# Second attention of a two-layer Perceiver block: where the picks, the first maximum and the last scores of a chunk stand

## The reference, cut to what matters

```python
x = x + _L0_xattn_ref(_layernorm(x), ctx_1024, mask, Wq, Wkv, Wo)
x = x + _L0_attn_ref(_layernorm(x), ...)      # gated delta net
x = x + _L0_ffn_ref(_layernorm(x), ...)       # top-1 of 8 experts
# the second attention, _L1_xattn_ref, H = 16 heads, d = 16:
q = (x_1 @ Wq.T + bq).reshape(1, 128, 16, 16).transpose(0, 2, 1, 3)
k = (x_2 @ Wk.T + bk).reshape(1, 12544, 16, 16).transpose(0, 2, 1, 3)
v = (x_2 @ Wv.T + bv).reshape(1, 12544, 16, 16).transpose(0, 2, 1, 3)
scores = einsum('bhqd,bhkd->bhqk', q, k) * 16 ** (-0.5)
out = einsum('bhqk,bhkd->bhqd', softmax(scores), v)
x = x + out
x = x + _L1_attn_ref(_layernorm(x), ...)      # linear attention with decay
x = x + _L1_ffn_ref(_layernorm(x), ...)       # top-2 of 8 experts
```

## Time and profile before

| what | value |
|---|---|
| three runs | 957.21, 960.98 (median), 963.67 us |
| profiled execution | 962.6 us, its span 960.8 us |
| mean granted TensorE clock | 0.984 of full speed |
| TensorE busy | 914.8 us of the span |
| VectorE, ScalarE, GpSimd busy | 709.1, 487.5, 300.2 us |
| second attention, first pick to last value matmul | 588.3 to 924.2 us |

### The profile page before, as it was taken

How to read it: one execution, slowest core, us unless ns; L and a number is a source line. 1 busy time by engine, 2 the same in 40 slices (tenths; PEclk the granted TensorE clock), 3 DMA queues, 4 the chain that set the end, 5 groups by cost and what they waited for, 6 DMA issues and landing times. The chain is left out here.

```text
span 960.8 us, 21439 instructions
## 1 busy us (share of the span) xinstructions
PE 914.8 (95%) x8224; PEld 575.9 (60%) x8224; DVE 709.1 (74%) x1216; ACT 487.5 (51%) x1156; POOL 300.2 (31%) x435
## 2 busy tenths in 40 slices
PE   7999999999999999888999989899999999999987
PEld 5444554455445445555778966566666666666775
DVE  3389778877887798988476625788787878878426
ACT  1543553355345534444386223266666666666743
POOL 4653355435442544356028114400000110000100
PEclk9999999999999999999999979999999999999999
DMA  8377847573557355632310049587766666666100
GB/s 168 132 201 204 226 187 183 136 202 140 130 135 200 127 140 136 159 115 98 106 45 1 2 124 215 138 243 182 178 172 185 161 161 161 167 170 186 48 3 6
DMA packets 103656, 136.33 MB, mean 142 GB/s; under 512 B 64153, under 2 KB 85425, under 8 KB 100881
## 3 DMA queue, kind: packets, MB, share of 16 engines
q1 hardware_dynamic: 99856, 134.22, 51.3%
q10 hardware_dynamic: 3712, 0.92, 0.6%
HBM read 81.48 MB, written 53.07 MB: 140 GB/s over the span
## 5 line engine op out<-in xcount | busy, mean ns | idle before, releaser
L1957 DVE TENSOR_REDUCE mx<-bank 128x1 f32<-128x896 f32 x224 | 233.8, 1085 | 58.3 <-PE bank L1808 55.4
L2018 ACT ACTIVATE p<-bank 128x512 f32<-128x512 f32 x392 | 204.3, 601 | 98.9 <-PE bank L1851 98.4
L699 DVE STREAM_TRANSPOSE ew<-sc 32x896 f32<-32x896 f32 x208 | 229.4, 1103 | 16.8 <-ACT sc L783 7.6
L561 PE MATMUL bank<-Wv,ctxT 128*128 128x512 f32 (+1 forms) x336 | 152.1, 586 | 0.4 <-ACT v L762 0.4
L1851 PE MATMUL bank<-qrows,krows 99*128 99x128 bf16 x1568 | 124.2, 220 | 5.5 <-ACT p L2018 4.8
L1851 PEld LDWEIGHTS bank<-qrows,krows 99*128 99x128 bf16 x1568 | 99.2, 97 | 42.6 <-ACT p L2018 9.7
L1808 PE MATMUL bank<-krows,qrows 96*128 96x512 bf16 x448 | 123.0, 356 | 1.4 <-issue 0.9
L1864 PE MATMUL bank<-p,v 128*32 128x128 f32 x3136 | 108.1, 276 | 4.4 <-issue 4.4
L561 PEld LDWEIGHTS bank<-Wv,ctxT 128*128 128x128 f32 x336 | 60.8, 190 | 79.0 <-issue 48.1
L1864 PEld LDWEIGHTS bank<-p,v 128*32 128x32 f32 x3136 | 80.3, 109 | 39.3 <-ACT p L2018 29.3
L443 POOL CAST kt<-kf 128x512 bf16<-128x512 f32 (+1 forms) x56 | 31.2, 558 | 218.4 <-ACT kf L755 218.4
(11 more groups left out here) (317 smaller groups left out, 1173.0 us busy)
## 6 DMA issues: line engine op xcount, KB each, us to landing
krows<-kscr SPq DMA_DIRECT2D x14, 1536.0 KB, 9.5
krows<-kscr SPq DMA_DIRECT2D x14, 1152.0 KB, 14.6
v<-vscr SPq DMA_DIRECT2D x14, 1004.5 KB, 12.8
vscr<-vpair SPq DMA_DIRECT2D x12, 1004.5 KB, 4.0
kscr<-kt SPq DMA_DIRECT2D x14, 768.0 KB, 3.6
kscr<-kt SPq DMA_DIRECT2D x14, 576.0 KB, 5.1
kscr<-kt SPq DMA_DIRECT2D x14, 512.0 KB, 4.5
ctxB<-ctx SPq DMA_DIRECT2D x56, 112.0 KB, 3.9
```

The lines of the kernel that those rows point to most:

```text
L561: ins = pe.matmul(bank[kv_bank(op, s)][:, 0:w * D], turned_context(c)[:, i, k * P:(k + 1) * P], Wv01[:, i, 0:w].rearrange("p w o -> p (w o)"),
L699: dve.transpose(pT0[j * SQ:(j + 1) * SQ, :, :, i * SQ:(i + 1) * SQ].rearrange("m t h q -> m h t q"), rows[:, j]).then_inc(S("turn0"), 1)
L1957: dve.tensor_reduce(mx1[:, c % 2, h:h + 1], psum[:, b:b + 2, :].rearrange("p b n -> p (b n)")[:, 0:CH], AX.X, ALU.max).then_inc(S("smread1 ...
L2018: act.activation(p1[:, g % PR, :], bank[ST1[g % 3]][:], ACT.Exp).then_inc(S("exp1"), 1)
```

## The change

SPLIT becomes 6, so that the loop scores ten heads one chunk ahead and six two chunks ahead; PLAN1 is written anew. PRO1 has three scores of chunk 1 ahead of the first M, not one, and three behind it, not seven. The third and fourth pick stand between the first scores; each pair of the first eight scores waits for its own cast. The first two late values stand behind the fourth score, with new banks and waits; the fillers begin later. GpSimd builds the mask behind the first maximum.

```diff
--- before.py
+++ after.py
@@ -1628,10 +1628,10 @@
         LATES = (LATE, NCH - 1)
         LU = 2 * CT
         LBANK = (4, 5, 7)
-        LAFTER = (0, 1, 3, 4, 6, 7, 9, 10, 12, 13, 15, 18, 20)
-        LATE_FIRST = 1 + sum(1 for n in LAFTER if n <= H1 + 1)
+        LAFTER = (4, 5, 7, 8, 10, 11, 13, 14, 16, 17, 18, 20)
+        LATE_FIRST = 2 + sum(1 for n in LAFTER if n <= H1 + 2)
         NPICK = 4
-        PBANK = (3, 6, 7, 0)
+        PBANK = (4, 5, 6, 7)
 
         moe0 = experts("moe0", a["L0_ffn_router_w"], True, a["L0_ffn_router_b"], a["L0_ffn_expert_b"], 1, False,
                 l1_loads, l1_clears,
@@ -1643,18 +1643,18 @@
         LB = (6, 7, 0, 1, 2)
         UNITS = CT * H1 // GH
         SLOTS = 3
-        SPLIT = 8
+        SPLIT = 6
 
 
 
         PLAN1 = (
-            (("S8",), ("S9",), ("R",)),
-            (("S10",), ("S11",), ("S12",)),
-            (("S13",), ("S14",), ("S15",)),
-            (("S0",), ("S1",), ()),
-            (("M",), ("S2",), ("S3",)),
-            (("S4",), ("S5",), ()),
-            (("S6",), ("S7",), ()))
+            (("S6",), ("S7",), ("R",)),
+            (("S8",), ("S9",), ("S10",)),
+            (("S11",), ("S12",), ("S13",)),
+            (("S14",), ("S15",), ("S0",)),
+            (("S1",), ("M",), ("S2",)),
+            (("S3",), ("S4",), ()),
+            (("S5",), (), ()))
 
         def plan1(c, t, k):
 
@@ -1671,7 +1671,7 @@
                     if d < NCH:
                         yield "S", d, h
 
-        PRO1 = tuple(("S", 0, h) for h in range(H1)) + (("S", 1, 0), ("M", 0, 0)) + tuple(("S", 1, h) for h in range(1, SPLIT))
+        PRO1 = tuple(("S", 0, h) for h in range(H1)) + (("S", 1, 0), ("S", 1, 1), ("S", 1, 2), ("M", 0, 0)) + tuple(("S", 1, h) for h in range(3, SPLIT))
         SMSEQ = PRO1 + tuple(op for c in range(NCH) for t in range(CT) for k in range(SLOTS) for op in plan1(c, t, k)) + (("R", NCH - 1, 0),)
         SMPOS = {op: i for i, op in enumerate(SMSEQ)}
 
@@ -1760,6 +1760,16 @@
                 pool.wait_ge(S("f1"), c + 1)
                 pool.tensor_tensor(acc1[:], acc1[:], bc(f1[:, c % 2, :], 2, [P, H1, D1 + 1]), ALU.mult).then_inc(S("acc1"), 1)
 
+            def block_mask():
+                pool.memset(blk16[:], 1.0).then_inc(S("blk16"), 1)
+                pool.wait_ge(S("blk16"), nth("blk16"))
+                v = blk16[:].rearrange("p (b u) -> p b u", u=DL)
+                pool.affine_select(out=v, in_=v, compare_op=ALU.is_ge, fill=0.0, base=0,
+                                              pattern=[[-DL, P // DL], [0, DL]], channel_multiplier=1).then_inc(S("blk16"), 1)
+                pool.wait_ge(S("blk16"), nth("blk16"))
+                pool.affine_select(out=v, in_=v, compare_op=ALU.is_ge, fill=0.0, base=DL - 1,
+                                              pattern=[[DL, P // DL], [0, DL]], channel_multiplier=-1).then_inc(S("blk16"), 1)
+
             make_picks(pool)
             ln_pool(pool, "ln2")
             pool.wait_ge(S("qpick_psum"), NPICK)
@@ -1770,18 +1780,12 @@
                 pool.memset(krows[half][KROWS:KONES].rearrange("p s h m -> p (s h m)").bitcast(F32),
                             TWO_ONES).then_inc(S("krows_ones"), 1)
                 pool.wait_ge(S("krows_ones"), half + 1)
-            pool.memset(blk16[:], 1.0).then_inc(S("blk16"), 1)
-            pool.wait_ge(S("blk16"), nth("blk16"))
-            v = blk16[:].rearrange("p (b u) -> p b u", u=DL)
-            pool.affine_select(out=v, in_=v, compare_op=ALU.is_ge, fill=0.0, base=0,
-                                          pattern=[[-DL, P // DL], [0, DL]], channel_multiplier=1).then_inc(S("blk16"), 1)
-            pool.wait_ge(S("blk16"), nth("blk16"))
-            pool.affine_select(out=v, in_=v, compare_op=ALU.is_ge, fill=0.0, base=DL - 1,
-                                          pattern=[[DL, P // DL], [0, DL]], channel_multiplier=-1).then_inc(S("blk16"), 1)
             for c in range(NCH):
                 maximum(c)
                 if c:
                     rescale(c - 1)
+                else:
+                    block_mask()
             rescale(NCH - 1)
 
         def second_tensor(pe):
@@ -1888,6 +1892,8 @@
                 b = LBANK[i % 3]
                 if i >= 3:
                     pe.wait_ge(S("v1late"), i - 2)
+                else:
+                    pe.wait_ge(S("qpicked"), (1, 2, NPICK)[i])
                 r, t = divmod(i, CT)
                 for k in range(DC):
                     ins = pe.matmul(bank[b][:, 0:D], (ctxT0, ctxL)[r][:, k, t * P:(t + 1) * P],
@@ -1896,7 +1902,7 @@
 
             def pick_rows(i):
 
-                pe.wait_ge(S("lT"), (0, 1, 2, 3)[i])
+                pe.wait_ge(S("lT"), (0, 0, 1, 2)[i])
                 for l in range(2):
                     for k in range(3):
                         ins = pe.matmul(bank[PBANK[i]][0:KROWS, l * D:(l + 1) * D], picks[:, 2 * i + l, k, :],
@@ -1905,16 +1911,21 @@
 
             pe.wait_ge(S("picks"), NJ + 1)
             pe.wait_ge(S("q3"), 3)
-            for i in range(NPICK):
-                pick_rows(i)
-            late_values(0)
+            pick_rows(0)
+            pick_rows(1)
             pe.wait_ge(S("lT"), len(LB))
-            pe.wait_ge(S("qpicked"), NPICK)
             for n, op in enumerate(PRO1):
+                if n < 8:
+                    pe.wait_ge(S("qpicked"), n // 2 + 1)
                 side(*op)
-                if n in LAFTER:
-                    late_values(LAFTER.index(n) + 1)
-                elif n > len(PRO1) - 7:
+                if n < 2:
+                    pick_rows(n + 2)
+                if n == 3:
+                    late_values(0)
+                    late_values(1)
+                elif n in LAFTER:
+                    late_values(LAFTER.index(n) + 2)
+                elif n > len(PRO1) - 5:
                     spin(pe, 6, 2)
             pe.wait_ge(S("v1late"), LU)
             for u in range(4):
```

## The result

| | before | after |
|---|---|---|
| median | 961.17 us (20 runs) | 964.67 us (20 runs) |
| lowest and highest of after | | 957.97 and 969.59 us |
| ratio, 95% interval | | 1.0035 [1.0018, 1.0052] |
| profiled execution, span | 962.6, 960.8 us | 969.27, 967.6 us |

The change costs 3.5 us, 0.35%, where the forecast was a gain of 0.3. The profiled execution of after is one of its longest (969.27 us; only one of the 20 was longer), so it shows more lost time than a usual one. What its single waits cost is therefore read from a second trace as well, and what a part of the change costs from the ratios of many executions.

The account below looks back on a forecast made before the run. TensorE, busy 914.8 of 960.8 us, was taken as the bound. Start -5.1, maximum's wait +2.7, late rows +0.8 and chunk 12 +1.3 gave -0.3 us: 960.7 us, range 954.5 to 966.

Parts of the forecast that it names:

- the picks between the scores: Prologue: first score 2.0 us earlier, fill 1.0 later, mask out of the way; first maximum's transpose moves 612.54 to 612.4.
- The start: Prologue: less work behind the first maximum's transpose, so the loop starts at 616.1, not 621.18: -5.1 us.
- If its clock falls: Prologue, behind TensorE's idle time before the first maximum's transpose: 1.4 us more if the clock falls; forecast took no fall.
- Chunk 0 of the loop: No term of its own; treated within chunks 0 to 11, each step +0.27 us, +2.7 in all, plus +0.8 for rows.
- A clean set of three: Loop, three row transfers of a chunk's maximum: 1.2 us between issues plus 1.8 landing, 3.0 us, in time.
- The room: Loop: from the start of the maximum's row transfers to the next chunk's first score group, 3.5 us.
- M's wait: Chunks 0 to 11: the maximum's transpose waits about 0.55 us on GpSimd; step +0.27 us, +2.7 in all.
- The rows of late chunks: Chunks 6 to 11: long row transfer sets stop TensorE 0 to 0.45 us each, +0.8 us in sum.
- Chunk 12: Two scores added and less work covering the maximum, whose transpose waits 0.9 to 1.2 us: together +1.3 us.
- Sum: Whole kernel: -5.1 + 2.7 + 0.8 + 1.3 = -0.3 us, so 960.7 us; chance 0.45.
- the rows come late in every chunk: Rival, each chunk's first score group: row sets of 3.95 us in all twelve cost 5.4, not 0.8; 965.3 us, chance 0.15.
- The start does not come early: Rival, prologue: clock falls after the shorter idle time, fill runs as before; start gains 3.7, 962.1 us, chance 0.18.

Follow-up runs that it names:

- picks and mask: Changed kernel with SPLIT, PLAN1 and PRO1 of the kernel before, leaving picks, banks, waits, late values and mask changed: 965.03 us, ratio 1.0025.
- after again: The changed kernel run once more without an edit, with a profile of another execution: 965.84 us, ratio 1.0034 to the kernel before.
- loop alone: Kernel before with only SPLIT, PLAN1 and PRO1 of the change; picks, late values, banks and mask as before: 962.04 us, ratio 0.9987.
- part 1: Changed kernel rerun unedited, then twice with the fetch of value slot 2 behind chunk 1's row transfers: 963.90 and 964.50 us, ratios 1.0028 and 1.0032.

## Why the prediction was wrong, point by point

- **The step that failed: the picks between the scores.** In the sum they stand at about nothing. The first score was to come 2.0 us earlier, held up only by the first cast and the copies of `lT`; the fourth pick and the fill behind it were to come 1.0 us later; the mask's 1.1 us were to pay for that; and the new banks and places of the late values were to "cost nothing". Measured, this part costs 4.6 us (2.3 to 6.9) over many executions. This is what was found in it. The 1.0 us was right, and M moved as forecast: 24.2 us behind the first pick before, 24.1 with picks and mask. But the start got 1.9 us longer, not 0. And the first score also needs the keys, which the prediction left out, since they had come in time before: it waited 0.46, 2.13, 2.59 and 3.53 us in four traces (the last with the keys made late on purpose), and since the fourth pick stands behind it, the fill and M moved along. These do not account for the whole 4.6 us.
- **The start** (-5.1): right in kind and size where nothing disturbed it: 27.8 to 28.2 us against 32.85, so -4.6 to -5.0. "If its clock falls": it didn't, in any of the traces with 1.1 to 1.3 us of idle time. But the loop's part alone, with the picks and the mask as before, has 27.92: the picks were not needed for it.
- **Chunk 0 of the loop**: a step that failed in the traces, though the times don't show its cost. "A clean set of three needs 1.2 + 1.8 = 3.0 us and is in time" was carried to the early chunks, with "all from chunk 6 on" for the long sets; the set of chunk 0 took 3.45 us already in the trace of before (636.91 to 640.36). In chunk 0 the loop had moved 5 us and the rows' issue 3.2 (48.6 us behind the first pick before, 45.4 in after again), and the fetch that waits for the store of late values had not moved (44.4 and 44.3). So the rows, issued 4.1 us behind that 1 MB before, are now issued 1.1 to 1.4 us behind it: landings of 3.1 to 5.8 us, a wait of 1.1 to 3.4 us in all six traces with the new loop and the fetch of slot 2 ahead of the rows, and in three of them half clock behind it. The room itself had shrunk as the prediction said (3.5 us), which is in part why before's loop, with landings of 3.4 to 3.9 us, waits 0.23. Yet the loop alone has this wait and no loss, and taking the wait away moved the ratio by 0.0002 to 0.0007.
- **M's wait** (0.55 a chunk): there, 0.31 to 0.34 in nine or more of the twelve chunks. The maximum's 3.7 us were right (3.6), the cover of 3.2 was 3.36. The shortest regular chunk is 21.41 or 21.42 us in five of the seven traces with the old loop and 21.60 to 21.62 in nine of the ten with the new: +0.2 against the forecast 0.27.
- **The rows of late chunks** (+0.8): 0.4 to 2.1 us in every trace with the new loop, most of it at the first groups of chunks 8 to 12, and 0 in every trace with the old.
- **Chunk 12** (+1.3): measured with the last chunk, 33.41 to 34.80, +1.4. Part of this agreement is luck: the cover without S0 and S1 is 3.2 - 0.86 = 2.3 us, not 2.5, and M waited 0.70 us, not 0.9 to 1.2.
- **Sum**: by the traces, -4.8 for the start, +2.3 for M, +0.4 to 2.1 for the rows, +1.4: between -0.7 and +1.0, as forecast. The loop alone bears it out: 0.9987, no loss. So the loop's sum held, and the +3.5 us of the whole change lie in the part that the sum had at nothing. Of the rivals, "the rows come late in every chunk" had the right sign; its reason, late sets in all twelve chunks, didn't occur, and late rows are not shown to be what the time went to. "The start does not come early" comes closest in kind, since the start lost 2 to 5 us in the three traces in which the first score waited over 2 us for the keys; but its condition, a fall of the clock behind the idle time at M, isn't what happened.

Not settled: what else in the picks part costs time; where the gain in the traces goes when the rows are no longer late (part 1); and why chunks 2 to 11 take 222.2 us in the loop alone and 224.1 to 226.9 in the other kernels with that loop (the gaps put down to "issue" in these chunks are 4.0 us there, 4.1 to 6.6 in the others). What lies behind those gaps no trace shows and no run tested.

## What to carry to other kernels

When a stage is moved earlier, go through every transfer that it or its neighbours issue and ask which of them moves along and which waits for something that doesn't: the order in the queue may stay, and the distance in it be gone. And a long fill that is off the path is better not released by work that can wait for a load: in the traces each late landing of the keys moved the fill, M and the start by about as much or more. A clean saving of 1.1 us (the mask) came out ahead of a change whose start was 5 us shorter.

Run each part of a change alone before explaining the whole from one trace. The longest wait in the trace of after, 3.4 us at the rows, was the easiest to explain and to remove, and removing it changed the time by nothing that could be measured; the part that the traces account for least made the difference.
